# The fill of ps_b: two transposes ahead of GpSimd's half, in a four-layer kernel with selective scans

## What is computed

```python
delta = softplus(...)                       # (b, s, 512)
dA  = exp(delta[..., None] * A)             # 16 states for each of 512 channels
dBu = delta[..., None] * Bm[:, :, None, :] * u[..., None]
h = dA_t * h + dBu_t                        # over 256 tokens
y = einsum('ben,bn->be', h, C_t)
```

## Time and profile before

| | us |
|---|---|
| median of 3 runs | 3688.07 |
| lowest, highest | 3681.33, 3688.27 |
| the profiled execution, its own time | 3710.73 |
| its span, first to last instruction | 3709.0 |

### The profile page before, as it was taken

One profiled execution on the slowest core, in us unless ns is written; L12 is line 12 of the kernel. 1 busy time (PEld: TensorE's weight loads), 2 busy tenths in 40 slices (PEclk: granted clock), 3 DMA queues, 4 the chain that ended last, 5 costly groups with the idle time before them and its releaser, 6 DMA issues.

```text
span 3709.0 us, 64650 instructions
## 1 busy us (share of the span) xinstructions
PE 3242.9 (87%) x22078; PEld 2674.0 (72%) x22078; DVE 2851.3 (77%) x3590; ACT 2921.7 (79%) x6624; POOL 2833.8 (76%) x3087
## 2 busy tenths in 40 slices
PE   6677788899999999999999999899989999897876
PEld 2556667787777878787877778787877777675643
DVE  1568778889797979798887979798888979793621
ACT  1658878888889898888888898988988898873522
POOL 0578989888898889888888888888888889780500
PEclk8899999999999999999999999999999999997866
DMA  4112222222122222212221222212221222220100
GB/s 170 59 51 82 80 66 65 85 65 88 61 87 63 83 63 80 74 59 89 65 87 58 82 69 79 71 60 89 63 88 60 87 61 78 60 69 19 44 2 10
DMA packets 140951, 257.08 MB, mean 69 GB/s; under 512 B 15921, under 2 KB 33329, under 8 KB 140225
## 3 DMA queue, kind: packets, MB, share of 16 engines
q1 hardware_dynamic: 140626, 252.95, 22.0%
HBM read 233.16 MB, written 5.05 MB: 64 GB/s over the span
## 4 chain that ended last, share of the span: by engine, by line
PE 48%; ACT 22%; DVE 11%; POOL 6%; issue 6%; DMA 0%; SPq 0%; POOLq 0%; DVEq 0%; ACTq 0%
PE ps_b L574 10%; PE ps_y L602 9%; ACT decay L639 8%; POOL g L693 5%; DVE hst L678 4%; PE ps_x L771 4%; ACT dbut L649 4%; PE ps_x L1276 3%; PE ps_x L765 3%; PE ps_v L765 3%; PE ps_x L1301 2%; PE ps_v L771 2%; PE ps_x L774 2%; PE ps_v L790 2%; ACT pT L1355 2%
## 5 line engine op out<-in xcount | busy, mean ns | idle before, releaser
L693 POOL TENSOR_TENSOR g<-hst,c_bc 128x512 f32<-128x512 f32 x1536 | 1976.1, 1287 | 482.2 <-PE ps_y L602 349.0
L678 DVE TENSOR_TENSOR_SCAN hst<-decay,ps_b 128x512 f32<-128x512 f32 x1536 | 1832.7, 1211 | 399.0 <-PE ps_b L574 231.8
L639 ACT ACTIVATE decay<-delta,acoef 128x256 f32<-128x256 f32 x3072 | 1378.4, 498 | 56.8 <-DVE hst L678 56.4
L574 PE MATMUL ps_b<-ident,dbut 128*128 128x128 f32 x6144 | 951.9, 278 | 241.4 <-DVE hst L678 110.3
L658 POOL TENSOR_TENSOR dbut<-dut,bcm 128x256 f32<-128x256 f32 x1536 | 972.4, 633 | 190.7 <-ACT dut L864 190.7
L602 PE MATMUL ps_y<-ident,g 128*128 128x128 f32 x6144 | 943.0, 276 | 20.8 <-ACT u L965 17.4
L574 PEld LDWEIGHTS ps_b<-ident,dbut 128*128 128x128 f32 x6144 | 708.0, 143 | 333.3 <-ACT dbut L649 165.1
L602 PEld LDWEIGHTS ps_y<-ident,g 128*128 128x128 f32 x6144 | 734.6, 142 | 147.4 <-issue 55.5
L649 ACT ACTIVATE dbut<-dut,bcm 128x256 f32<-128x256 f32 x1536 | 767.4, 500 | 22.0 <-PE ps_b L574 18.8
L1355 ACT ACTIVATE pT<-ps_x 128x1024 f32<-128x1024 f32 x128 | 129.5, 1012 | 74.5 <-PE ps_x L1311 64.3
L1301 PE MATMUL ps_x<-qT,kT 18*128 18x256 f32 x1024 | 159.6, 433 | 16.7 <-ACT pT L1355 15.6
(11 more groups left out here) (192 smaller groups left out, 4080.3 us busy)
## 6 DMA issues: line engine op xcount, KB each, us to landing
c_bc<-c_rows SPq DMA_DIRECT2D x768, 256.0 KB, 3.2
rows_bc<-mod_rows SPq DMA_DIRECT2D x16, 384.0 KB, 4.4
ada_w<-in_ada_w_dram SPq DMA_DIRECT2D x1, 5120.0 KB
weights<-in_weights_dram SPq DMA_DIRECT2D x1, 4832.0 KB, 34.8
x<-in_x_dram SPq DMA_DIRECT2D x16, 256.0 KB, 3.8
x0p<-x SPq DMA_DIRECT2D x16, 256.0 KB, 2.3
xr<-x SPq DMA_DIRECT2D x16, 256.0 KB, 2.3
x<-x SPq DMA_DIRECT2D x16, 256.0 KB, 3.6
```

The lines of the kernel that those rows point to most:

```text
L574: last = nc.tensor.matmul(ps_b[:, u % 2, e * T + t * P:e * T + (t + 1) * P], dbut[:, u % NDBU, t, e * P:(e + 1) * P], ident[:, :], is_tran ...
L639: last = nc.scalar.activation(decay[:, u % (DA_AHEAD + 2), e, :], delta[s][:, eb, :], ACT.Exp, scale=acoef[:, s, eb, n:n + 1])
L678: nc.vector.tensor_tensor_scan(line(hst[:, u % NHST, :, :].rearrange("p e t -> p (e t)")), line(decay[:, u % (DA_AHEAD + 2), :, :].rearran ...
L693: nc.gpsimd.tensor_tensor(g[:, u % NG, :, :], hst[:, u % NHST, :, :], c_bc[:, k % NCB * CHUNK + n % CHUNK, :].unsqueeze(1) .broadcast_to([ ...
```

## The change

A fill of ps_b had three waits ahead of its four transposes: ACT's half (dbu_a), GpSimd's half (dbu_p), then the bank (scan_done). Now it waits for the bank, then for ACT's half, makes the two transposes that read ACT's half (t = 0), then waits for GpSimd's half and makes the other two. The loops over e and t change places, so that both transposes of one half stand together; the last transpose is the same one as before, and b_full is counted there as before. A second edit moves VectorE's wait for the modulation rows (row_in) from ahead of the first norm's statistics to just ahead of the scaling that reads them.

```diff
--- before.py
+++ after.py
@@ -565,12 +565,11 @@
 
             def spread_b(self, pe, u):
 
-                pe.wait_ge(S["dbu_a"], u + 1)
-                pe.wait_ge(S["dbu_p"], u + 1)
                 if u >= 2:
                     pe.wait_ge(S["scan_done"], u - 1)
-                for e in range(HALF):
-                    for t in range(TB):
+                for t, made in enumerate(("dbu_a", "dbu_p")):
+                    pe.wait_ge(S[made], u + 1)
+                    for e in range(HALF):
                         last = nc.tensor.matmul(ps_b[:, u % 2, e * T + t * P:e * T + (t + 1) * P],
                                                 dbut[:, u % NDBU, t, e * P:(e + 1) * P], ident[:, :],
                                                 is_transpose=True, start=True, stop=True)
@@ -907,7 +906,6 @@
         def l0_in_vector(dve, ch, b, at):
             yield next(at)
             dve.wait_ge(S["x_in"], nth("x_in", b, 16))
-            dve.wait_ge(S["row_in"], nth("row_in", b, 16))
 
             def modulate(t, mean, inv):
                 ch.done(nc.vector.scalar_tensor_tensor(out=xa[:, t, :], in0=x0[:, t, :], scalar=mean,
@@ -917,6 +915,7 @@
 
             norm_stats(ch, b, "a1", x0)
             yield next(at)
+            dve.wait_ge(S["row_in"], nth("row_in", b, 16))
             ch.done(norm_scale(dve, b, "a1", modulate))
             norm_stats(ch, b, "a2", xa)
             yield next(at)
```

## The result

The changed kernel takes 3731.98 us (median of 4 runs, 3723.3 to 3744.96) against 3688.17 for the kernel before (4 runs, 3681.33 to 3690.99). The ratio is 1.0122, with a 95% interval of 1.0094 to 1.0149: 44 us slower, where 14 us faster was forecast. The profiled execution took 3744.96 us, its span is 3743.3 us (3709.0 before).

The account below looks back on a forecast made before the run. No engine is full; hand-overs bound the kernel, with 48% of the chain on TensorE, whose fills wait for GpSimd's half. 15 batches x 1.3 = 19.5 us plus 1.0 give 20.5; two thirds, 14 us, gives 3674 us, range 3660 to 3689.

Parts of the forecast that it names:

- The ends are 0 and 20.5: Bounds on the whole kernel's gain in us, from no place paying to every place paying in full; 14 taken.
- work of the engines meets differently, which no row prices: Unpriced way to be slower, anywhere in the kernel; slower by over 0.2% for any reason had chance 0.10.
- Two transposes early, 0.22 us a late fill: ps_b fills held only by GpSimd's half: two transposes done beforehand bring TensorE and b_full 0.22 us earlier.
- the other five ... 5 x 0.22 = 1.1 us a batch: Five of six chain fills per batch that waited for GpSimd, followed by queued TensorE work, gain 1.1 us a batch.
- rival (b): After late fills, another path was due as early; only prologue and one or two fills pay: 4.8 us, chance 0.23.
- the 8 us at which the forecast began: Low end of the main forecast for the whole kernel, 8 to 20 us less, 3668 to 3680 us; chance 0.58.
- The order of the waits, 0.06 us: Scan's wait rides on the fill's first weight load: 0.06 us at three fills, 0.2 us a batch.
- what would show it: List of trace signs for right or wrong, among them L571's separate wait instruction showing 51 ns nearly always.
- row_in, 1.0 us in the prologue: VectorE's first statistics start 1.1 us earlier, near 76.4; net gain 1.0 us, nothing in later batches.
- Rival (d): Wait inside each fill delays the third load, costing up to 51 ns; at that, 22 us slower, 3710; chance 0.04.
- Rival (c): TensorE's queue freed at L571 and VectorE's waits for the fill shortened too: 30 us less, 3658; chance 0.09.

Follow-up runs that it names:

- fill_only: Kernel before with only the new fill, two transposes ahead of GpSimd's half, the wait for the rows unmoved: 3728.86 us, 1.0092 of before.
- order_only: Kernel before with only the order of the three waits changed, bank first, all ahead of the four transposes: 3688.88 us, 0.9984 of before.
- after_pause: Changed kernel with GpSimd waiting, at one unit of each batch, for a sum_states one unit later than it needs: 3681.85 us, 0.9949 of before.
- before_place: Kernel before, old fill, with four TensorE matmuls (L771, first output projection of layer L1) placed one tick later: 3738.56 us, 1.01 of before.
- after_normb: Changed kernel with the cols1 copy on ACT, L3's norm d2 reading PSUM and L1's norm b scaled on ACT: 3621.87 us, 0.9808 of before.
- before_normb: Kernel before with the cols1 copy on ACT, L3's norm d2 reading PSUM and L1's norm b scaled on ACT: 3625.39 us, 0.9812 of before.

## Why the prediction was wrong

**The step that failed is in the sum: "The ends are 0 and 20.5".** A TensorE that comes earlier was taken to be worth its 0.22 us or nothing, because the next meeting might be due anyway. It can also cost, and the cost isn't bound by the 0.22 (44 us in all were lost): taking 0.2 us from TensorE took a 0.11 us pause from GpSimd, which added 2.0 us to a copy on VectorE and, in batches with a lower granted clock, 1.2 to 3.0 us more. fill_only and order_only place the loss in the early transposes, after_pause and before_place show the pause to be the cause.

The sentence on slower cases named it in kind ("work of the engines meets differently, which no row prices") and was wrong that no row prices it. The trace of before had the row: one copy of 4.14 us, with a window of granted clock 0.62 behind it, beside thirteen of 1.8, one of 0.57 and one of 0.16. Such a spread of one instruction of one shape is a price list. The copy alone is 2.3 us over the usual; from its start (479.48) to the end of GpSimd's wait (494.21) that batch took 14.73 us for 9.51, 5.2 more. 13 batches at 2.3 to 5.2 us give 30 to 68 us, and 44 was measured; what the row could not have told is that the pause would be lost.

**Two transposes early, 0.22 us a late fill: right locally.** The timeline of the changed kernel:

```profile
1294.25 0.63 POOL L657 TENSOR_TENSOR dbut<-dut,bcm 128x256 f32<-128x256 f32 x1
...
1294.94 0.44 PE L573 MATMUL ps_b<-ident,dbut 128*128 128x128 f32 x2 [0.48 <-POOL dbut L657]
```

From the end of GpSimd's half to the end of the fill's transposes it is 0.50 us (1294.88 to 1295.38), where the earlier trace rows give 0.74 (1291.08 to 1291.82).

**"... the other five ... 5 x 0.22 = 1.1 us a batch": its size is not shown.** In after_normb against before_normb the new fill gained 3.5 us between the medians, 0.2 us in each of 15 batches: one fill of five, near rival (b), for which the prediction took 4.8 us. With five runs of each, which scatter by 17 and 20 us, neither no gain nor the 8 us at which the forecast began is excluded; nor is that pair free of the other effect, since a scaling that still reads x takes 410 ns in the median with the old fill and 699 with the new. after_pause, 0.5% below before, leaves open that the whole gain is there. The waits show the trade: from before_normb to after_normb, VectorE's wait for the fill fell from 218.3 to 199.5 us and its wait for GpSimd's g rose from 59.1 to 85.2. What became of each of the other four fills was not followed.

**The order of the waits, 0.06 us: right in the mechanism, not to be seen in the time.** The separate instruction at L571 now lasts 51 ns each time, as "what would show it" had it. From the end of the scan to the fill the chain has 0.04 us, where the earlier trace rows have 0.14. The shift is 0.10 us, the upper end of what was taken. order_only's interval of 0.9959 to 1.0009 neither shows nor excludes the 3 us.

**row_in, 1.0 us in the prologue: as worked out.** Statistics from 76.45 in place of 77.56, and the first scaling at 78.17, where before had it at 79.20. The profile puts VectorE's wait of 0.68 us ahead of the scaling down to the rows; nearly all of it is the inverse root on ACT, which ended at 78.05:

```profile
76.45 0.75 DVE L727 BATCH_NORM_STATS2 stats<-x 128x6 f32<-128x256 f32 x2 [4.41 <-DMA x<-in_x_dram]
...
77.85 0.20 ACT L738 ACTIVATE nrm<-nrm 128x2 f32<-128x2 f32 x1
78.17 0.48 DVE L911 SCALAR_TENSOR_TENSOR xa<-x,mv,rows_bc 128x256 f32<-128x256 f32 x1 [0.68 <-DMA rows_bc<-mod_rows]
```

**Rival (d), the right sign for the wrong reason.** No hole opens inside a fill: with GpSimd's half long there, its four loads still take the 0.47 us of the earlier trace rows, and the third load follows the second after 109 ns in the median, as before. **Rival (c)** fell with the rest: VectorE's wait for the fill did not shrink in the changed kernel, it grew.

## What to carry to other kernels

Before an engine is brought forward, list the instructions whose longest time is a multiple of their shortest for the same shape. They wait inside themselves for something that no list of waits names, and here what let them through was another engine's pause; the longest one in the trace of before is the price if the pause goes. Small SBUF-to-SBUF work of VectorE beside a GpSimd that works without a gap is such a case: with its input in PSUM (d2, 1.6% of the whole kernel) it was cheaper though slower at its best. On ACT the copy no longer cost the changed kernel its 1.2%; in the kernel before, the same move earned nothing clear of noise. And count the gap that such a wait opens on TensorE twice: here the granted clock fell behind it in 11 batches of 13.

## What the runs showed of the hardware

A 128x4 copy of VectorE within SBUF took 0.16 us without GpSimd and 3.83 us beside it, and a 128x256 scaling 0.40 and up to 4.43 us; the long ones (the copy's from 1.8 us on, the scaling's of 4.4) lasted through two or more instructions of GpSimd and ended with a pause of it. The same scaling with its input in PSUM took 0.52 to 0.54 us. The Trainium skill describes the contention in "SBUF — State Buffer", section "SBUF: two separate sides": GpSimd shares a port pair with VectorE instructions in a mode that uses two ports or with two SBUF inputs, and whichever starts first has it for its whole instruction, while the other is fully blocked; it counts an fp32 copy within SBUF to the former. The trace agrees that the copy is blocked, but the loser doesn't have its turn at the next instruction: in the changed kernel the copy was issued at 1300.09 and GpSimd ended the multiply then running and four more instructions before it was done. A pause isn't the only way in, though. Two other copies of the same shape, here the one at L1410 in the trace of before, run beside a GpSimd that doesn't pause either:

```profile
1375.30 0.63 POOL L658 TENSOR_TENSOR dbut<-dut,bcm 128x256 f32<-128x256 f32 x1
1375.64 0.32 DVE L1410 COPY cols<-mod_cols 128x4 f32<-128x4 f32 x1
1375.87 1.30 POOL L693 TENSOR_TENSOR g<-hst,c_bc 128x512 f32<-128x512 f32 x1
```

It was issued 0.34 us into GpSimd's multiply and ended 0.03 us after it, and so it went in 12 of the 13 batches in which it runs beside scan units; in the other it took 3.92 us. The copy of this study was issued 0.07 us into a g before the change and 0.43 us into the multiply after it, 0.21 us ahead of its end, and had to wait for a pause both times. What decides whether VectorE gets in between two instructions stays open; no run moved only the time at which it asks.

Where a wait rides also has a price. With the scan's wait on the first weight load, the fill starts 0.04 us after the scan in the chain; through the separate instruction it was 0.14.
